# Holding back GpSimd's gathers until the other engines have moved on, in a macaron block (expert FFN, scan, expert FFN)

## The chip, the cores and the metric

The kernel runs on one core of one Trainium2 chip. The metric is device time in microseconds (us) of one execution, given as the median of three runs. All times below are from the kernel before the change.

## The reference

The block is x + 0.5·FFN(norm x), then x + Attn(norm x), then x + 0.5·FFN(norm x) again, with the same FFN weights, on 4 × 512 tokens of 256 floats. The FFN has a shared expert and 16 routed ones of width 176, of which each token uses four.

```python
def _L0_ffn_ref(x, ...):
    scores = jax.nn.sigmoid(logits) + gate_b
    weights, indices = jax.lax.top_k(scores, 4)
    weights = weights / weights.sum(-1, keepdims=True)
    shared_out = jax.nn.silu(x @ w1_shared) * (x @ w3_shared) @ w2_shared
    ...
    h3 = jax.nn.silu(h1 * h2)
    experts_out = jnp.einsum('btec,ecd->bted', h3, w2_routed)
    routed_out = jnp.einsum('bted,bte->btd', experts_out, router_probs)
    return shared_out + routed_out
# _L0_attn_ref: xp = x W_in; dt = softplus(xp W_dt + b); a = exp(-dt exp(log_A));
# y_t = a_t * y_(t-1) + xp_t over the 512 tokens; output y W_out
x = x + 0.5 * _L0_ffn_ref(_layernorm(x, axis=-1), ...)
x = x + _L0_attn_ref(_layernorm(x, axis=-1), ...)
x = x + 0.5 * _L0_ffn_ref(_layernorm(x, axis=-1), ...)
```

## The kernel before, in words

Tokens stand in 16 token tiles of 128 rows (`NT`), resident in SBUF as `xres`. Each of the two FFN layers (`f` = 0 and 1) has the same stages. The block is written out by hand for five engines: each engine has its own program, in the order of the code, and they meet only at semaphores. Nothing reorders it.

**Routing.** The tokens are normed, written to DRAM (`xn_scratch`), and sorted by expert into at most 79 slot tiles (`NS`) of 128 rows, each for one expert.

**The loop over 79 slot tiles** (`pipeline`). GpSimd gathers the rows of slot tile j with an indirect DMA into one of `UN` = 4 buffers (`gather`, L555). TensorE transposes them (L1387, counted by `s_xt`, "x_transposed"), multiplies by the expert's up weights (L1365, counted by `s_h`), transposes the hidden values (L1426 and L1427) and multiplies by the down weights (L1416). In one step c of its pipeline TensorE does, in this order: transpose of tile c, up product of tile c−1, down product of tile c−4, hidden transposes of tile c−2. ScalarE's step holds, in order: the first copy of hidden values (L671, counted by `s_a`, "hidden_first"), the copy of transposed hidden values (L662), of transposed rows (L653), the silu (L702) and the copy of the output (L681). VectorE forms the products and the low halves of the operands. SyncE writes each output tile to DRAM (`ys_scratch`).

**Early rows.** A token tile's result is the weighted sum of four rows of `ys_scratch` per token. For the first 8 token tiles this is begun inside the loop: from gather 29 on, behind every second gather, GpSimd also issues one `fetch_early` (L567), 25 of 32 in the loop and 7 behind it. VectorE adds them to `xres` (L1100, counted by `s_ea`).

**Behind the loop** GpSimd runs `combine` for the other 8 token tiles, t = 8 to 15, here called k = 0 to 7: four gathers each (L580), 32 in all. In layer 0 the scan part (called mamba in the code) runs beside them on the other engines, in 9 chunks c of two or one token tiles: ScalarE norms (L854), TensorE transposes (L1574, `m_s["xt"]`), ScalarE copies (L862, then `xin`), TensorE multiplies (L1582, `m_s["xp"]`), ScalarE copies (L868), TensorE multiplies (L1582, `m_s["z"]`), then ScalarE's chain of functions, VectorE's scan and TensorE's output product (L1607). There are six rooms for the gathered rows, so k = 6 and 7 wait for VectorE's additions (L1143, counted by `s_cd`). In layer 1, what runs beside the gathers is the shared expert's down part, in 8 pairs of token tiles: TensorE transposes (L1491, `s_st`), ScalarE copies (L752, counted by `s_hs`), TensorE multiplies (L1502, `s_sy`), VectorE adds (L1165), and VectorE adds the gathered rows (L1143). There each k has a room of its own, and the gathers wait for nothing but their first release. Each finished token tile goes out by a DMA.

A gather waits in GpSimd's own program, so everything behind it in that program waits too.

Of the kernel before, what the change touches and what calls it, by code (L numbers as in the profile page):

```python
# [12 lines left out]
NT = N // P  # L13
# [7 lines left out]
UN = 4  # L21
NS = NSLOT_MAX
NT_TE = -(-NS // UN) * UN
STEPS = NT + NS
# [14 lines left out]
ROOMS = 6  # L39
# [2 lines left out]
MEASURED = 5  # L42
SCALED = ((0, 4), (4, EARLY_TILES))
TABLE_AFTER = 76
SH_BEFORE, SH_ENDS = 2, 11
HID_AHEAD = 6
SUMS_AFTER = {9: (0, 1), 10: (2,), 11: (3,), 12: (4,), 13: (5,), 14: (6, 7)}
# [34 lines left out]
def build(nc, x_d, w13r_d, w2r_d, w13s_d, w2s_d, wm_d, cst_d, hcst_d, out_d):  # L82
# [7 lines left out]
    with ctx:  # L90
# [431 lines left out]
        def _(pool):  # L522
# [28 lines left out]
            def gather(f, j):  # L551

                if j >= UN:
                    pool.wait_ge(s_xt, f * STEPS + NT + j - UN + 1)
                pool.indirect_dma_start(xg[j % UN], None, xn_dram,  # L555
                                        bass.IndirectOffsetOnAxis(ap=tokidx[:, j:j + 1], axis=0)
                                        ).then_inc(s_g[j % UN], 16)

            def fetch_early(f, n):

                t, q = divmod(n, TOPK)
                if q == 0:
                    for b in range(2):
                        pool.wait_ge(s_yw[b], written(f, b, tiles_before(t)))
                if n >= ROWS:
                    pool.wait_ge(s_ea, f * EARLY + n - ROWS + 1)
                pool.indirect_dma_start(early_rows[n % ROWS], None, ys_dram[0:tiles_before(t) * P, :],  # L567
                                        bass.IndirectOffsetOnAxis(ap=si[:, n:n + 1], axis=0)
                                        ).then_inc(s_er[n % ROWS], 16)

            def combine(f, t):

                for b in range(2):
                    pool.wait_ge(s_yw[b], written(f, b, tiles_before(t)))
                if f == 0 and t >= EARLY_TILES + ROOMS:
                    pool.wait_ge(s_cd, combined_to(f, t - ROOMS))
                for q in range(TOPK):
                    n = t * TOPK + q
                    room = cgl[t - EARLY_TILES] if f else cg[(t - EARLY_TILES) % ROOMS]
                    pool.indirect_dma_start(room[:, q, :], None, ys_dram[0:tiles_before(t) * P, :],  # L580
                                            bass.IndirectOffsetOnAxis(ap=si[:, n:n + 1], axis=0)
                                            ).then_inc(gathered(f, t, q)[0], 16)
# [1083 lines left out]
```

## Time and profile before

| what | us |
|---|---|
| median of three runs | 677.86 (675.02 to 683.16) |
| the profiled execution | 680.63 |
| its span in the trace | 678.7 |
| TensorE busy in it | 523.3 (77%) |
| VectorE busy | 444.3 (65%) |
| ScalarE busy | 374.9 (55%) |
| GpSimd busy | 350.3 (52%) |

In the trace PE is TensorE, DVE is VectorE, ACT is ScalarE, POOL is GpSimd and SP is SyncE. A row of a timeline gives start, duration, engine, line, operation, what is written and read, how many instructions were merged, and in brackets the idle time of the engine before it and what ended it. "remote" there, and "another core or an unknown queue" in the chain, mean that a semaphore was reached at a time at which the trace knows no instruction that ended. Ends of matmuls are modelled.

### The profile page before, as it was taken

What the parts mean: (1) busy time and instruction counts of PE and PEld (TensorE: products, weight loads), DVE (VectorE), ACT (ScalarE), POOL (GpSimd) and SP (SyncE); (2) the same over time, 40 slices, a digit from 0 to 9 for tenths busy, and PEclk for the clock granted to TensorE, in tenths of its full rate; (3) what the DMA queues carried; (4) which work ended last, traced back from release to release, by engine and by line L of the source; (5) the groups of instructions that cost most, each with busy time, mean ns of one, the idle gap of its engine ahead of it and who ended that gap; (6) DMA issues with size and microseconds to landing.
All of it is one profiled execution on the core that took longest, in us unless ns stands there. A gap on an engine that the chain in (4) does not pass through costs nothing.

```text
span 678.7 us, 13762 instructions
## 1 busy us (share of the span) xinstructions
PE 523.3 (77%) x3206; PEld 459.5 (68%) x3207; DVE 444.3 (65%) x1461; ACT 374.9 (55%) x1128; POOL 350.3 (52%) x362
## 2 busy tenths in 40 slices
PE   4965869999999997645686932699999999978424
PEld 3843569998888887524574921499988888867313
DVE  6789747777676765513987589477666666745514
ACT  2764747766566664435575553477666666644000
POOL 3895564466565653571402323544565665644770
PEclk9977679999999998786898965699999999979655
DMA  9951135565544443431200450254444445545541
GB/s 299 393 218 47 48 111 170 157 174 151 162 132 145 136 135 98 128 107 32 63 0 17 154 187 0 63 149 140 132 141 138 146 133 145 129 114 155 160 120 67
DMA packets 61141, 88.17 MB, mean 130 GB/s; under 512 B 9499, under 2 KB 46363, under 8 KB 61107
## 3 DMA queue, kind: packets, MB, share of 16 engines
q1 hardware_dynamic: 47379, 50.29, 21.6%
q0 software_dynamic: 13728, 37.50, 21.3%
q8 instruction: 12, 0.20, 0.1%
q14 instruction: 22, 0.18, 0.1%
HBM read 57.22 MB, written 30.54 MB: 129 GB/s over the span
## 4 chain that ended last, share of the span: by engine, by line
PE 60%; DVE 12%; another core or an unknown queue 10%; ACT 8%; issue 6%; DMA 2%; POOL 1%; ACTq 0%; SPq 0%; DVEq 0%
PE bank L1365 26%; PE bank L1416 12%; PE bank L1387 6%; PE bank L1426 4%; PE bank L1427 4%; PE bank L1582 3%; PE bank L1502 2%; ACT ring_f L702 1%; PE bank L1607 1%; PE bank L1438 1%; DVE xres L1143 1%; DMA ring_f<-xn_scratch,tokidx 1%; DMA raw_shared<-in_w13s 1%; DVE stage L998 1%
## 5 line engine op out<-in xcount | busy, mean ns | idle before, releaser
L555 POOL DMA_INDIRECT ring_f<-xn_scratch,tokidx x158 | 152.5, 965 | 148.7 <-PE bank L1387 106.7
L1365 PE MATMUL bank<-w_routed,ring_r 128*128 x948 | 196.4, 343 | 0.0
L1365 PEld LDWEIGHTS bank<-w_routed,ring_r 128*128 128x128 f32 x948 | 153.3, 193 | 4.6 <-issue 2.8
L1416 PE MATMUL bank<-w_routed,ring_r 128*128 x790 | 120.1, 282 | 1.0 <-ACT ring_f L681 0.6
L1416 PEld LDWEIGHTS bank<-w_routed,ring_r 128*128 128x128 f32 x790 | 110.9, 189 | 1.8 <-issue 1.8
L662 ACT ACTIVATE ring_r<-bank 128x256 fp32r<-128x256 f32 x158 | 60.6, 384 | 63.3 <-PE bank L1427 51.1
L671 ACT ACTIVATE stage<-bank 128x176 f32<-128x176 f32 x158 | 50.4, 319 | 54.6 <-PE bank L1365 28.7
L947 DVE TENSOR_TENSOR ring_r<-bank,ring_r 128x128 fp32r<-128x128 f32 x158 | 45.3, 287 | 51.8 <-ACT ring_r L662 50.6
L580 POOL DMA_INDIRECT mamba_room<-ys_scratch,si x64 | 61.0, 953 | 33.1 <-issue 19.6
L939 DVE TENSOR_TENSOR ring_r<-bank,ring_r 128x256 fp32r<-128x256 f32 x158 | 67.0, 424 | 15.8 <-ACT ring_r L653 8.6
L1387 PE MATMUL bank<-cst,ring_f 128*128 128x128 f32 x316 | 64.9, 288 | 14.6 <-DMA ring_f<-xn_scratch,tokidx 10.4
L524 POOL TENSOR_TENSOR w_routed<-raw_routed,w_routed 128x512 fp32r<-128x512 f32 (+1 forms) x36 | 54.2, 1539 | 33.6 <-ACT w_routed L637 33.6
L653 ACT ACTIVATE ring_r<-bank 128x256 fp32r<-128x256 f32 x158 | 60.4, 383 | 19.9 <-issue 9.8
L956 DVE TENSOR_TENSOR ring_f<-bank,stage 128x48 f32<-128x48 f32 x158 | 32.6, 206 | 59.0 <-ACT stage L671 44.9
L702 ACT ACTIVATE ring_f<-ring_f 128x240 f32<-128x240 f32 x158 | 63.6, 402 | 0.3 <-DVE ring_f L957 0.2
L681 ACT ACTIVATE ring_f<-bank 128x256 f32<-128x256 f32 x158 | 60.0, 380 | 4.1 <-DMA ys_scratch<-ring_f 2.1
L1426 PE MATMUL bank<-cst,ring_f 128*128 128x128 f32 x158 | 46.3, 293 | 18.5 <-ACT ring_f L702 13.2
L1582 PE MATMUL bank<-mamba_room,stage 128*128 128x256 f32 (+1 forms) x144 | 39.1, 423 | 26.6 <-ACT mamba_room L862 15.6
L1387 PEld LDWEIGHTS bank<-cst,ring_f 128*128 128x128 f32 x316 | 38.3, 145 | 25.8 <-issue 13.5
L1582 PEld LDWEIGHTS bank<-mamba_room,stage 128*128 128x128 f32 x144 | 28.8, 221 | 35.5 <-ACT mamba_room L862 16.2
L957 DVE TENSOR_TENSOR ring_f<-bank,stage 128x176 f32<-128x176 f32 x158 | 52.1, 330 | 0.0
L949 DVE TENSOR_TENSOR ring_r<-bank,ring_r 64x128 fp32r<-64x128 f32 x158 | 46.5, 294 | 2.1
(172 smaller groups left out, 836.2 us busy)
## 6 DMA issues: line engine op xcount, KB each, us to landing
ys_scratch<-ring_f SPq DMA_DIRECT2D x158, 128.0 KB
raw_routed<-in_w13r SPq DMA_DIRECT2D x6, 704.0 KB, 12.1
xn_scratch<-w_routed SPq DMA_DIRECT2D x32, 128.0 KB, 4.5
raw_routed<-in_w2r SPq DMA_DIRECT2D x6, 512.0 KB, 12.9
raw_routed<-in_w13r SPq DMA_DIRECT2D x8, 352.0 KB, 6.2
ring_f<-xn_scratch,tokidx POOLq DMA_INDIRECT x158
xres<-in_x_in SPq DMA_DIRECT2D x4, 512.0 KB, 7.1
raw_routed<-in_w2r SPq DMA_DIRECT2D x8, 256.0 KB, 7.2
```

Of the source, the lines that this page charges most:

```text
L555: pool.indirect_dma_start(xg[j % UN], None, xn_dram, bass.IndirectOffsetOnAxis(ap=tokidx[:, j:j + 1], axis=0)).then_inc(s_g[j % UN], 16)
L580: pool.indirect_dma_start(room[:, q, :], None, ys_dram[0:tiles_before(t) * P, :], bass.IndirectOffsetOnAxis(ap=si[:, n:n + 1], axis=0)).th ...
L653: act.activation(xT[b][0], p_xT[b][:, 0:DC * P], ACT.Copy).then_inc(s_xhi, 1)
L662: act.activation(hT[b][0], p_hT[b][:, 0:2 * P], ACT.Copy).then_inc(s_hhi, 1)
L681: act.activation(yb[b], p_y[b][:, 0:D], ACT.Copy).then_inc(s_yo, 1)
L702: act.activation(hid[c % 2][:, 0:HD + HB], hid[c % 2][:, 0:HD + HB], ACT.Silu).then_inc(s_s, 1)
L939: dve.tensor_tensor(xT[b][1], p_xT[b][:, 0:DC * P], xT[b][0].bitcast(f32), ALU.subtract).then_inc(s_xlo, 1)
L1365: last = pe.matmul(out, a, b, start=(q == 0), stop=(q == len(terms) - 1))
L1387: last = pe.transpose(p_xT[b][:, q * P:(q + 1) * P], xg[k][:, q * P:(q + 1) * P], ident)
L1416: last = pe.matmul(p_y[b][:, 0:D], a, v, start=(q == 0), stop=(q == 4))
L1426: pe.transpose(p_hT[b][:, 0:P], hid[b][:, 0:P], ident)
L1582: last = pe.matmul(out[:, part(c, e)], m_w[m][:, q * D + e * P:q * D + (e + 1) * P], src[:, part(c, q)], start=(q == 0), stop=(q == DC - 1))
```

## The change

GpSimd gets more to wait for, at three places. No instruction is added, removed or moved on any engine.

1. In the loop, each gather j from 30 on also waits until `s_a` has reached j − 4, that is, until ScalarE's first copy of slot tile j − 5 is done. A `fetch_early` inside the loop waits for the same count as the gather ahead of it (for the first, that of gather 29).
2. Behind the loop of layer 0, the gathers of k = 1 to 5 each also wait for the scan part: k = 1 for the first chunk transposed, k = 2 for the first `xp`, k = 3 for the first `z`, k = 4 for the second `z`, k = 5 for the third `xp`.
3. Behind the loop of layer 1, those of k = 2 to 7 also wait for ScalarE's copy of pair k − 2 of the shared hidden values (`s_hs` at k − 1), and from k = 3 on for VectorE to have added all rows of k − 3.

```diff
+MAMBA_FIRST = {1: ("xt", 1), 2: ("xp", 1), 3: ("z", 1), 4: ("z", 2), 5: ("xp", 3)}
...
                 if j >= UN:
                     pool.wait_ge(s_xt, f * STEPS + NT + j - UN + 1)
+                if j > EARLY_FIRST:
+                    pool.wait_ge(s_a, f * STEPS + NT + j - UN)
...
                 if n >= ROWS:
                     pool.wait_ge(s_ea, f * EARLY + n - ROWS + 1)
+                if early_after(n) < NS:
+                    pool.wait_ge(s_a, f * STEPS + NT + early_after(n) - UN)
...
-                if f == 0 and t >= EARLY_TILES + ROOMS:
-                    pool.wait_ge(s_cd, combined_to(f, t - ROOMS))
+                k = t - EARLY_TILES
+                if f == 0:
+                    if k in MAMBA_FIRST:
+                        reached, chunks = MAMBA_FIRST[k]
+                        pool.wait_ge(m_s[reached], chunks)
+                    if k >= ROOMS:
+                        pool.wait_ge(s_cd, combined_to(f, t - ROOMS))
+                elif k >= 2:
+                    pool.wait_ge(s_hs, k - 1)
+                    if k >= 3:
+                        pool.wait_ge(s_cd, combined_to(f, t - 3))
```

GpSimd's program in the loop of layer 0, at the first early rows, before (`ring_f` is the buffer of a slot tile's rows; `stage` and `lg` are rooms of early rows):

```order
L555 DMA ring_f<-xn_scratch,tokidx 128x256 [waits x_transposed] x26
L567 DMA stage<-ys_scratch,si 128x256 [waits y_written1,y_written0]
L555 DMA ring_f<-xn_scratch,tokidx 128x256 [waits x_transposed] x2
L567 DMA stage<-ys_scratch,si 128x256
L555 DMA ring_f<-xn_scratch,tokidx 128x256 [waits x_transposed] x2
```

and the same place after:

```order
L558 DMA ring_f<-xn_scratch,tokidx 128x256 [waits x_transposed] x26
L572 DMA stage<-ys_scratch,si 128x256 [waits hidden_first,y_written1,y_written0]
L558 DMA ring_f<-xn_scratch,tokidx 128x256 [waits hidden_first,x_transposed] x2
L572 DMA stage<-ys_scratch,si 128x256 [waits hidden_first]
L558 DMA ring_f<-xn_scratch,tokidx 128x256 [waits hidden_first,x_transposed] x2
```

The order is the same; every transfer behind the first 30 gathers has a wait more, for ScalarE's count.

GpSimd's program behind the loop of layer 0, k = 0 to 5, before (`mamba_room` holds the gathered rows):

```order
L580 DMA mamba_room<-ys_scratch,si 128x256 [waits y_written1,y_written0,y_sums]
L580 DMA mamba_room<-ys_scratch,si 128x256 x3
L580 DMA mamba_room<-ys_scratch,si 128x256 [waits y_written1,y_written0]
L580 DMA mamba_room<-ys_scratch,si 128x256 x3
L580 DMA mamba_room<-ys_scratch,si 128x256 [waits y_written1,y_written0]
```

and after:

```order
L594 DMA mamba_room<-ys_scratch,si 128x256 [waits y_written1,y_written0,y_sums]
L594 DMA mamba_room<-ys_scratch,si 128x256 x3
L594 DMA mamba_room<-ys_scratch,si 128x256 [waits m_xt,y_written1,y_written0]
L594 DMA mamba_room<-ys_scratch,si 128x256 x3
L594 DMA mamba_room<-ys_scratch,si 128x256 [waits m_xp,y_written1,y_written0]
L594 DMA mamba_room<-ys_scratch,si 128x256 x3
L594 DMA mamba_room<-ys_scratch,si 128x256 [waits m_z,y_written1,y_written0]
L594 DMA mamba_room<-ys_scratch,si 128x256 x3
L594 DMA mamba_room<-ys_scratch,si 128x256 [waits m_z,y_written1,y_written0]
```

Here too nothing moved: the first gather of each four has a wait more, on a count of TensorE.

## Rows read from the trace of the kernel before

**Rows 1.** The page: busy time by engine, and the chain's shares.

```profile
PE 523.3 (77%) x3206; PEld 459.5 (68%) x3207; DVE 444.3 (65%) x1461; ACT 374.9 (55%) x1128; POOL 350.3 (52%) x362
...
PE 60%; DVE 12%; another core or an unknown queue 10%; ACT 8%; issue 6%; DMA 2%; POOL 1%; ACTq 0%; SPq 0%; DVEq 0%
```

**Rows 2.** The waits: us in total, times, longest.

```profile
ACT raw_ring L752 <- remote: 33.2, 2, 25.3
...
DVE xres L1165 <- remote: 18.3, 2, 16.1
...
ACT mamba_room L862 <- remote: 16.7, 1, 16.7
```

**Rows 3.** Windows, L671 alone (one per slot tile): length, busy (count), PEclk, DMA share, GB/s.

```profile
441.00:481.00 40.00, 6.38 (x20) 1.00 0.49 142
500.00:590.00 90.00, 11.96 (x38) 1.00 0.48 139
...
160.00:250.00 90.00, 12.06 (x38) 1.00 0.50 145
```

**Rows 4.** Timeline of GpSimd in the loop of layer 1.

```profile
520.14 0.95 POOL L555 DMA_INDIRECT ring_f<-xn_scratch,tokidx  x1 [1.28 <-PE bank L1387]
521.39 0.95 POOL L567 DMA_INDIRECT stage<-ys_scratch,si  x1 [0.30 <-issue]
522.64 0.95 POOL L555 DMA_INDIRECT ring_f<-xn_scratch,tokidx  x1 [0.30 <-issue]
524.86 0.94 POOL L555 DMA_INDIRECT ring_f<-xn_scratch,tokidx  x1 [1.27 <-PE bank L1387]
```

**Rows 5.** The same stretch, TensorE and ScalarE.

```profile
523.40 0.27 PE L1427 MATMUL bank<-cst,ring_f 128*128 128x128 f32 x1
523.51 0.38 PE L1387 MATMUL bank<-cst,ring_f 128*128 128x128 f32 x2
...
523.65 1.22 PE L1365 MATMUL bank<-w_routed,ring_r 128*128 x6
524.66 0.38 ACT L662 ACTIVATE ring_r<-bank 128x256 fp32r<-128x256 f32 x1 [1.27 <-PE bank L1427]
...
525.76 0.33 ACT L671 ACTIVATE stage<-bank 128x176 f32<-128x176 f32 x1
```

**Rows 6.** Timeline of GpSimd behind the loop of layer 0: gathers 1, 16 and 24.

```profile
279.55 0.94 POOL L580 DMA_INDIRECT mamba_room<-ys_scratch,si  x1 [0.30 <-issue]
...
298.32 0.95 POOL L580 DMA_INDIRECT mamba_room<-ys_scratch,si  x1 [0.30 <-issue]
...
308.33 0.94 POOL L580 DMA_INDIRECT mamba_room<-ys_scratch,si  x1 [0.30 <-issue]
```

**Rows 7.** The same stretch, TensorE and ScalarE.

```profile
293.14 1.99 PE L1582 MATMUL bank<-mamba_room,stage 128*128 128x256 f32 x8 [1.27 <-ACT mamba_room L868]
295.31 0.66 PE L1574 MATMUL bank<-cst,mamba_room 128*128 128x128 f32 x4 [0.17 <-ACT mamba_room L854]
...
311.92 0.60 ACT L862 ACTIVATE mamba_room<-bank 128x512 f32<-128x512 f32 x1 [16.66 <-remote]
```

**Rows 8.** Timelines of TensorE, ScalarE, VectorE and GpSimd, end of layer 1.

```profile
629.79 0.60 PE L1491 MATMUL bank<-cst,mamba_room 128*88 128x128 f32 x4
...
658.07 3.78 PE L1502 MATMUL bank<-raw_shared,raw_ring 88*128 88x256 f32 x8 [18.05 <-issue]
...
666.54 7.19 PE L1502 MATMUL bank<-raw_shared,raw_ring 88*128 88x256 f32 x16 [3.84 <-ACT raw_ring L752]
...
657.42 0.59 ACT L752 ACTIVATE raw_ring<-bank 88x512 f32<-88x512 f32 x1 [25.33 <-remote]
665.90 1.08 ACT L752 ACTIVATE raw_ring<-bank 88x512 f32<-88x512 f32 x2 [7.88 <-remote]
...
647.68 2.05 DVE L1143 SCALAR_TENSOR_TENSOR xres<-mamba_room,wk,xres 128x256 f32<-128x256 f32 x4
...
656.21 0.95 POOL L580 DMA_INDIRECT mamba_room<-ys_scratch,si  x1 [0.30 <-issue]
```

## Prediction

> **What bounds the kernel now.** I read the page first. TensorE is busy for 77% of the span and carries 60% of the chain, but 10% of the chain, some 67 us, belongs to no instruction the trace knows [rows 1]. The waits say where the long pieces of it are: ScalarE's L752 and VectorE's L1165 near the end, and ScalarE's L862 in the scan part, each for 16 to 25 us at a stretch and ended by "remote" [rows 2]. All three wait on TensorE. The reader is to ask whether TensorE was late, and it was not. In the scan part its transposes L1574 ended at 295.97, and ScalarE, idle since 295.26, copied their result at 311.92, 16 us later [rows 7]. Near the end the transposes L1491 ended at 630.39 and their copy began at 657.42, 27 us later [rows 8].
>
> Next I looked at what ran meanwhile. In the first stretch GpSimd issued 24 gathers without a break, 1.25 us apart, the last ending at 309.27, and ScalarE came free 2.65 us after that [rows 6, 7]. In the loop the same stands small. A slot tile takes 2.00 us while GpSimd issues one gather for each, and 2.37 us once every second gather has an early row behind it, in both layers [rows 3]. A pair then takes 4.74 us instead of 4.00. In it GpSimd issues three transfers in a row, 520.14 to 523.59 [rows 4]. TensorE's hidden transposes ended at 523.67, and ScalarE took them at 524.66, 1.07 us after GpSimd had stopped; GpSimd itself, which waited for transposes that ended at 523.89, went on at 524.86 [rows 4, 5]. So my reading: while GpSimd issues gathers back to back, TensorE's progress reaches the others late, and it comes through some 1 to 2.6 us after GpSimd pauses. The trace shows the coincidence, not the cause.
>
> **Part 1, the loop.** The gate adds a wait and no work. Before, a pair was three transfers (3.45 us from first start to last end), 1.07 us until TensorE's progress was seen, and 0.20 us until GpSimd went on: 4.72, which fits the 4.74. Queued behind a gated gather on GpSimd are the next early row and gather; TensorE waits for them only if the four buffers run dry, and a gather is needed four steps, 8 us, after the transpose that freed its room.
> The gain at most: if the pauses fall so that nothing is seen late, the pair returns to 4.00. Tiles 25 to 72 are 24 pairs in each layer, so 0.74 × 24 × 2 = 35.5 us. The loss: the gate needs ScalarE's copy behind the up product, a 0.33 us instruction [rows 5], instead of TensorE's transpose. If that product too is seen 1.07 us after GpSimd stops, the pair is 3.45 + 1.07 + 0.33 + 0.30 (the shortest gap between two transfers, taken for the way back [rows 4]) = 5.15, so 0.41 × 48 = 20 us more. Between them lies a mixture. Three transfers every 4.00 us leave GpSimd a pause of only 0.55 us, less than the 1.07 that followed a row of three, which speaks against a full cure; TensorE can run ahead of a longer pair, which speaks against the full loss. I take 0, nearest to the row of before, and keep −35 and +20.
>
> **Part 2, behind the loop of layer 0.** GpSimd's k = 0 to 3 end at 299.27 [rows 6]; what k = 1 to 3 wait for (the first chunk) is done well before. k = 4 needs the second z, whose matmuls ended at 295.13 [rows 7], but GpSimd learns that as late as ScalarE does. So I expect GpSimd to stop at 299.27, TensorE's progress to come through at most 2.65 us later, and ScalarE's L862 to start at 301.9 instead of 311.92: 10.0 us earlier. From this I take 1 us off, because k = 4 and 5 now run beside the next chunk, where before GpSimd was silent, and a row of three cost 1.07. That is −9. If z is seen promptly, the gate holds only at k = 5 (third xp, which needs the stalled L862): GpSimd stops 5 us later, at 304.3, and the gain is 5. If pauses free nothing, it is 0. What the gate delays costs nothing: k = 4 and 5 are added two and more chunks later, and k = 6 and 7 waited for additions already. Bounds −10 and 0.
>
> **Part 3, behind the loop of layer 1.** Seven of the eight gates are open in time in the timeline of before: for the closest of those of VectorE, k = 7 starts at 656.21 and VectorE had added k = 4 at 649.73 [rows 8]. The copy that k = 7 asks for (pair 5) began at 657.42. GpSimd stops at 655.9, and the copy, now freed within 1 to 2.6 us of that, stays near 657.4 to 658. The gathers of k = 7 start about 2 us later. But the silence frees the copy of pair 6 too, which before came only at 665.90, since its transposes were long done. TensorE's last three products are then one row: from 658.1, 3.78 us for pair 5, 1.06 for the last transposes at that pace, and 7.19 for pairs 6 and 7 [rows 8], ending at 670.1. Before, they ended at 673.73. So −3.6. Bounds: −8 if ScalarE is freed as early as 653, +2 if only the 2 us of delay are left.
>
> **A rule against the change.** GpSimd's gathers share the DMA engines with everything else, and those are busy for 0.48 to 0.49 of the time in the quick stretch and in the slow one alike [rows 3]. The Trainium skill, "DMA: Bandwidth & Descriptors", section "SWDGE vs HWDGE vs iDMA", says that queues fed by software and by hardware are separate inside each DMA engine and served in turn. By that, gathers cannot shut others out of the engines, and spacing them frees no transfer: the time would be that of the second rival below. The trace agrees on the equal DMA share; it does not say whether semaphores suffer in another way.
>
> **The sum.** 0 − 9 − 3.6 = −12.6 us on the profiled execution, 680.63 to 668.0 (its span 678.7 to 666.1). The median of the three runs stands 2.8 us below that execution, so the forecast is 665.3, rounded to 665.
>
> **The rivals.**
> - *The loop is cured in part or in whole.* For it speaks that the pair was 4.00 us with single gathers [rows 3], and that the gate stops GpSimd exactly when ScalarE is behind. Against it: the 0.55 us pause. Half the cure is −18 on top: 647. The whole is 630.
> - *The pauses free nothing.* The late semaphores have another cause, which only happens to end near GpSimd's pauses; the copy at 657.42 came while GpSimd was still issuing [rows 8], which speaks for it. Then the gates hold a little here and there behind work that is late anyway: 677.9, give or take 3. Against it are the 1.07 us in the loop, at every pair.
> - *The gate feeds back and the kernel is slower.* At the loop's third transfer, TensorE's up product is seen late, ScalarE's copy follows, and only then the next gather: 5.15 us a pair. That costs 20 us and outweighs the 12.6: 685. It decides from 0.26 us more a pair (12.6 / 48). For it speaks that GpSimd has no slack to give (three transfers 1.25 us apart in a pair of 4.00); against it, that TensorE has 8 us of buffers.
>
> Also possible is that a gate simply never holds, since GpSimd asks for counts that are nearly always reached; in parts 2 and 3 that is the second rival.
>
> **How the numbers follow.** The forecast 0.42, the cure 0.20, nothing freed 0.20, the feedback 0.18. The range goes half way into the cure's values and up to the feedback's, 642 to 684; the forecast's own is 656 to 672. A measurement of this kernel can tell about 1%, 6.8 us, from no change. Faster by more: 0.38 of the forecast's 0.42, the cure's 0.20 and 0.04 of the second rival, 0.62. Slower by more: 0.16 of the feedback and 0.02 of the second, 0.18. Within 1%: the rest, 0.20.
>
> **What would show it.** In the changed profile, L862's 16.7 us and L752's 33.2 us under "remote" should fall to a few us each; a pause of GpSimd should stand ahead of k = 4 in layer 0 and ahead of k = 7 in layer 1, and ScalarE's wait should end 1 to 2.6 us into it. The count of L671 in 90 us of the loop tells part 1: 38 is no change, 45 the cure, 35 the feedback. If the count moves by more than 1, part 1's zero was wrong. If GpSimd pauses and ScalarE still waits over 5 us into the pause, my reading of the cause is wrong.

## The result, and the profile after

| | us |
|---|---|
| changed kernel, median | 710.95 (702.01 to 716.08, 4 runs) |
| kernel before, beside it | 679.63 (675.02 to 683.16, 4 runs) |
| ratio | 1.0365, 95% interval 1.0311 to 1.0419 |
| profiled execution of the changed kernel | 707.15, its span 705.3 |

The ratio and its interval compare the kernel before with the changed kernel's 702.01 and 707.15 alone, since 714.75 and 716.08 fell in a slower state that some executions of either kernel can show; the median of 710.95 takes in all four. By the ratio the kernel became 3.7% slower. The forecast was 665, so the sign was wrong. The rival that came true is the third, the gate that feeds back. Lines in the changed file stand 14 further down for TensorE, ScalarE and VectorE (L671 is L685), and GpSimd's gathers are L558 (loop), L572 (early rows) and L594 (behind the loops).

The page of the changed kernel, against [rows 1]:

```profile
PE 524.7 (74%) x3206; PEld 468.4 (66%) x3207; DVE 446.8 (63%) x1461; ACT 374.9 (53%) x1128; POOL 350.9 (50%) x362
...
PE 56%; DVE 12%; another core or an unknown queue 11%; issue 9%; ACT 8%; DMA 2%; POOL 1%; ACTq 0%; SPq 0%; DVEq 0%; POOLq 0%
```

The work is the same to within 3 us on every engine (TensorE's weight loads, PEld, which overlap its products, have 8.9 us more), and the span is 26.6 us longer: nearly all of it is waiting. From the first to the last of ScalarE's first copies, the loop of layer 0 takes 191.8 us in place of 177.8, that of layer 1 193.6 in place of 179.4; what lies between the loops takes 1.7 us less, and what follows the last copy takes the same (63.5 and 63.4). So the loops, 28.2 us longer together, have more than all of it. The windows, L685 alone, against [rows 3]:

```profile
441.00:481.00 40.00, 5.39 (x17) 0.90 0.44 126
500.00:590.00 90.00, 10.47 (x33) 0.92 0.40 120
160.00:250.00 90.00, 10.74 (x34) 0.98 0.44 129
```

Where 38 slot tiles went by in 90 us, now 33 or 34 do: 2.7 us each in place of 2.37, in both layers. (The first window lies in the stretch of single gathers and has 17 in place of 20 only because the loop of layer 1 now begins at 448.23; the single gathers still come 2.00 us apart.) The prediction set 35 for the feedback and 38 for no change. The waits:

```profile
POOL ring_f L558 <- ACT stage L685: 39.9, 21, 2.0
...
ACT ring_r L676 <- remote: 32.7, 10, 4.3
...
ACT raw_ring L766 <- remote: 37.6, 3, 21.9
...
DVE xres L1179 <- remote: 16.1, 2, 15.9
...
ACT mamba_room L882 <- remote: 14.2, 2, 10.5
```

The first is the new gate, but only a part of it: a wait for several counts is put down to the one that the profile sees last. Held against ScalarE's copies one by one, 55 of the 98 gathers with the new wait start 0.74 to 0.76 us after the end of just the copy that they ask for, and these are all that waited at all; some stand in the profile as waits for TensorE. The second, ScalarE's copy of transposed hidden values in the loop, was this before:

```profile
ACT ring_r L662 <- remote: 9.1, 2, 5.8
```

The third and fourth are the waits of the last stage, 33.2 and 18.3 us before [rows 2], and together they have not shrunk.

One turn of the loop shows the feedback. GpSimd in the late loop of layer 1:

```profile
532.78 0.95 POOL L558 DMA_INDIRECT ring_f<-xn_scratch,tokidx  x1 [1.95 <-ACT stage L685]
534.04 0.95 POOL L572 DMA_INDIRECT stage<-ys_scratch,si  x1 [0.30 <-issue]
535.29 0.95 POOL L558 DMA_INDIRECT ring_f<-xn_scratch,tokidx  x1 [0.30 <-issue]
538.09 0.95 POOL L558 DMA_INDIRECT ring_f<-xn_scratch,tokidx  x1 [1.85 <-ACT stage L685]
539.34 0.94 POOL L572 DMA_INDIRECT stage<-ys_scratch,si  x1 [0.30 <-issue]
540.59 0.95 POOL L558 DMA_INDIRECT ring_f<-xn_scratch,tokidx  x1 [0.30 <-issue]
541.84 0.95 POOL L558 DMA_INDIRECT ring_f<-xn_scratch,tokidx  x1 [0.30 <-issue]
543.09 0.95 POOL L572 DMA_INDIRECT lg<-ys_scratch,si  x1 [0.30 <-issue]
547.14 0.94 POOL L558 DMA_INDIRECT ring_f<-xn_scratch,tokidx  x1 [3.10 <-PE bank L1401]
```

and the copy that the gate asks for, with the product ahead of it on TensorE:

```profile
534.02 1.23 PE L1379 MATMUL bank<-w_routed,ring_r 128*128 x6
...
537.02 0.32 ACT L685 ACTIVATE stage<-bank 128x176 f32<-128x176 f32 x1 [1.97 <-remote]
...
544.49 0.38 ACT L676 ACTIVATE ring_r<-bank 128x256 fp32r<-128x256 f32 x1 [3.59 <-remote]
...
546.08 0.32 ACT L685 ACTIVATE stage<-bank 128x176 f32<-128x176 f32 x1
```

The up product ended at 535.25, while GpSimd was between two transfers. GpSimd's row of three ended at 536.24, and only 0.78 us after that did ScalarE take the product. Its copy ended at 537.34, and the next gather started 0.75 us later. So the pair took 3.46 (the row) + 0.78 + 0.32 + 0.75 = 5.31 us, the sum of the rival with its terms a little shifted (3.45 + 1.07 + 0.33 + 0.30). After a pause the opposite comes: counts that have piled up let five transfers through in a row (538.09 to 544.04). While they run ScalarE waits 3.59 us for TensorE's hidden transposes and takes them 0.45 us after the row; its next first copy ends at 546.40, and 0.74 us later GpSimd goes on, at 547.14. The profile names TensorE for that wait of 3.10 us, but the time is the gate's. Three slot tiles have then taken 9.05 us, where 7.1 were usual. The gates do not spread the transfers. They bunch them.

### The profile page after: what moved, and what is told of

The parts are those of the page before. It is cut to its first block, busy times and chain, and to the rows that moved or that the text cites. A ratio compares the mean times of both kernels' runs of the same rounds, so it can differ in the third digit from the quotient of the medians.

```text
span 705.3 us, 13903 instructions
## 1 busy us (share of the span) xinstructions
PE 524.7 (74%) x3206; PEld 468.4 (66%) x3207; DVE 446.8 (63%) x1461; ACT 374.9 (53%) x1128; POOL 350.9 (50%) x362
## 4 chain that ended last, share of the span: by engine, by line
PE 56%; DVE 12%; another core or an unknown queue 11%; issue 9%; ACT 8%; DMA 2%; POOL 1%; ACTq 0%; SPq 0%; DVEq 0%; POOLq 0%
PE bank L1379 24%; PE bank L1430 13%; PE bank L1401 5%; PE bank L1440 3%; PE bank L1441 2%; PE bank L1596 2%; ACT ring_f L716 2%; PE bank L1516 2%; DMA ring_f<-xn_scratch,tokidx 1%; DVE lg L933 1%; PE bank L1621 1%; DMA raw_shared<-in_w13s 1%; DVE stage L1012 1%; ACT ring_r L667 1%
## 5 line engine op out<-in xcount | busy, mean ns | idle before, releaser
L558 POOL DMA_INDIRECT ring_f<-xn_scratch,tokidx x158 | 153.0, 969 | 182.0 <-PE bank L1401 101.4
L1379 PE MATMUL bank<-w_routed,ring_r 128*128 x948 | 201.9, 350 | 4.4 <-issue 2.8
L1379 PEld LDWEIGHTS bank<-w_routed,ring_r 128*128 128x128 f32 x948 | 158.1, 199 | 10.9 <-issue 9.8
L1430 PE MATMUL bank<-w_routed,ring_r 128*128 x790 | 123.6, 288 | 0.7 <-DVE ring_r L963 0.6
L1430 PEld LDWEIGHTS bank<-w_routed,ring_r 128*128 128x128 f32 x790 | 114.4, 195 | 1.6 <-issue 1.6
L685 ACT ACTIVATE stage<-bank 128x176 f32<-128x176 f32 x158 | 50.1, 317 | 46.1 <-PE bank L1379 26.4
L594 POOL DMA_INDIRECT mamba_room<-ys_scratch,si x64 | 61.3, 958 | 23.2 <-issue 19.0
L1596 PE MATMUL bank<-mamba_room,stage 128*128 128x256 f32 (+1 forms) x144 | 36.9, 405 | 26.8 <-issue 13.9
L1440 PEld LDWEIGHTS bank<-cst,ring_f 128*128 128x128 f32 x158 | 22.5, 142 | 48.7 <-ACT ring_f L716 45.8
L1401 PEld LDWEIGHTS bank<-cst,ring_f 128*128 128x128 f32 x316 | 40.3, 148 | 16.8 <-DMA ring_f<-xn_scratch,tokidx 12.3
```

What stands on the lines that cost most here:

```text
L558: pool.indirect_dma_start(xg[j % UN], None, xn_dram, bass.IndirectOffsetOnAxis(ap=tokidx[:, j:j + 1], axis=0)).then_inc(s_g[j % UN], 16)
L1379: last = pe.matmul(out, a, b, start=(q == 0), stop=(q == len(terms) - 1))
L1401: last = pe.transpose(p_xT[b][:, q * P:(q + 1) * P], xg[k][:, q * P:(q + 1) * P], ident)
L1430: last = pe.matmul(p_y[b][:, 0:D], a, v, start=(q == 0), stop=(q == 4))
L1440: pe.transpose(p_hT[b][:, 0:P], hid[b][:, 0:P], ident)
L1596: last = pe.matmul(out[:, part(c, e)], m_w[m][:, q * D + e * P:q * D + (e + 1) * P], src[:, part(c, q)], start=(q == 0), stop=(q == DC - 1))
```

## What the experiments were to tell apart

The kernel before took 677.9 to 686.8 us in some groups of runs and 602 in others. The groups of experiments fell on four numbered chips (that of the first profiles is not on record). Chip 1 gave the same time in both of its groups; the other three had one group each, so that it is the chip, and not the hour, rests on these five groups. Each comparison below is within one group.

| chip | kernel before | runs on it |
|---|---|---|
| 12 | 686.83 (684.39 to 689.59) | e1 to e4 |
| 9 | 602.71 (600.43 to 607.51) | e5 to e8 |
| 1 | 679.09 (673.16 to 682.31) | f1 to f4 |
| 2 | 601.63 (600.92 to 605.50) | g1 to g4 |
| 1 | 680.53 (673.21 to 681.54) | h1, h2 |

On chips 12 and 1, as in the profiles above, single waits ended by "remote" last up to 28.9 us (e1, e3 and e4) and up to 19.8 (f1). In the eight profiles from chips 9 and 2 the views of waits have no "remote" at all. I call the first two late chips and the others prompt chips.

## Which part of the change costs

**e1_loop_gates**, the change without its parts behind the loops:

```diff
+                if j > EARLY_FIRST:
+                    pool.wait_ge(s_a, f * STEPS + NT + j - UN)
...
+                if early_after(n) < NS:
+                    pool.wait_ge(s_a, f * STEPS + NT + early_after(n) - UN)
```

> Only the gates inside the two loops, none behind them. Feedback theory (ScalarE's copy lies behind TensorE's late progress, so each row of transfers starts later): both loops as long as in the changed kernel, 14 us more each than before, slot tiles 2.65 to 2.75 us apart instead of 2.37, total +26 to +30 us against before. Rival (the gates behind the loops cost the time, or the loop only lengthens together with them): under +10 us.

**e2_behind_gates**, the change without these two waits.

> Only the gates behind the loops. Feedback theory: loops as before (178 and 179 us from first to last copy). Behind the loop of layer 0 the gate at the fifth group of four stops GpSimd and frees ScalarE, but the sixteen gathers then issued in a row hold it again: -5 to +2 us; layer 1 unchanged within 2 us. Total -6 to +3. Rival (part 2 works as I forecast and only the loop spoilt the result): -8 to -13 us.

**e3_looser**, e1 with the count one lower in both (`- UN - 1`), so that the copy asked for is one slot tile older.

> Loop gates alone, each asking for one copy less (that of slot tile j-6 instead of j-5). Feedback theory: that copy is done before GpSimd would start anyway, so the gate hardly holds: within 5 us of before. Rival (any extra wait on GpSimd costs, whatever it asks for): as much as the loop gates as they are, +20 or more.

**e4_rows_gate**, e1 with the gate on the early rows alone, none on the gathers.

> Of the loop gates only those of the early rows are left; the gathers of slot tiles are free. Feedback theory: the early row still waits for the copy and stands between two gathers, so most of the loss stays, though not at each gather: +8 to +20 us. Rival (the loss comes from the slot tiles' gathers reaching TensorE too late): 0 to +4.

| | median us | ratio, 95% interval | both loops in the profile, us |
|---|---|---|---|
| e1_loop_gates | 724.09 (722.18 to 725.72) | 1.0543 (1.0507 to 1.0579) | 395.6 |
| e2_behind_gates | 679.19 (677.26 to 687.22) | 0.9908 (0.9875 to 0.9940) | 361.5 |
| e3_looser | 701.43 (701.19 to 703.05) | 1.0204 (1.0172 to 1.0237) | 377.8 |
| e4_rows_gate | 691.73 (688.81 to 694.54) | 1.0060 (1.0032 to 1.0088) | 371.6 |

The last column adds the two loops, each from its first to its last first copy; e2's are without a gate. The loop's gates cost 37 us alone, more than the 26 to 30 that I had expected, and 34 of them stand in the loops' own length. The gates behind the loops give back 6 by the ratio and 8 by the medians, between e2's two expectations (6 at most by the one, 8 at least by the other). Together that is 30, near what the change cost on chip 1 (32 and 30 us by the ratios below; 25 in its first group). e4 costs 4 us by the ratio, where I had expected 8 to 20, though its profile, of its slowest execution, has loops 10 us longer: two of the three transfers of a pair are free of the gate there, so the early rows' gate is the small part and the gathers' the large one. For e3 I had expected little or no cost, and it costs 14 us. GpSimd in its late loop says why:

```profile
526.03 0.94 POOL L558 DMA_INDIRECT ring_f<-xn_scratch,tokidx  x1 [1.02 <-PE bank L1392]
527.28 0.95 POOL L572 DMA_INDIRECT stage<-ys_scratch,si  x1 [0.30 <-issue]
528.53 0.95 POOL L558 DMA_INDIRECT ring_f<-xn_scratch,tokidx  x1 [0.30 <-issue]
531.61 0.94 POOL L558 DMA_INDIRECT ring_f<-xn_scratch,tokidx  x1 [2.13 <-ACT stage L676]
...
541.84 0.94 POOL L558 DMA_INDIRECT ring_f<-xn_scratch,tokidx  x1 [2.12 <-ACT stage L676]
```

The gate still holds, but in every second pair: two pairs take 10.2 us (531.61 to 541.84) where two of [rows 4] take 9.48. One copy of slack halves how often the loop closes and does not open it.

## Are the gathers what makes TensorE late?

**e5_rows_by_memset** and **f3_rows_by_memset** are one kernel. Every early row is zeros from GpSimd, so the early rows' sums are left out:

```diff
-                pool.indirect_dma_start(early_rows[n % ROWS], None, ys_dram[0:tiles_before(t) * P, :],
-                                        bass.IndirectOffsetOnAxis(ap=si[:, n:n + 1], axis=0)
-                                        ).then_inc(s_er[n % ROWS], 16)
+                pool.memset(early_rows[n % ROWS], 0.0).then_inc(s_er[n % ROWS], 16)
```

**e6_late_by_memset** and **f4_late_by_memset** do the same to the gathers behind both loops, and leave out those sums:

```diff
-                    pool.indirect_dma_start(room[:, q, :], None, ys_dram[0:tiles_before(t) * P, :],
-                                            bass.IndirectOffsetOnAxis(ap=si[:, n:n + 1], axis=0)
-                                            ).then_inc(gathered(f, t, q)[0], 16)
+                    pool.memset(room[:, q, :], 0.0).then_inc(gathered(f, t, q)[0], 16)
```

> The kernel before, with one edit: each early row (64 in all, 50 of them in the loops) is filled with zeros by a memset on GpSimd instead of being gathered, so the early rows' sums are left out; VectorE's additions of them stay. Theory (TensorE's progress is seen late while GpSimd issues gathers one behind the other): the rows of three gathers are gone, the pair of slot tiles returns from 4.74 toward 4.00 us, the count of L671 in 90 us of the late loop goes from 38 to 44 or 45, and the kernel is 25 to 36 us shorter, some 650 on the median of before. Rival A (VectorE's additions of the early rows, or GpSimd being busy with anything, slow the loop): the count stays at 38 to 39, and the time falls by under 8 us, through the 14 gathers behind the loops that no longer stand ahead of the others. Rival B (the data that the early rows move is what slows the loop): as the theory in time, but then the count would also be below 45 in the early part of the loop where the transfers share is the same, 0.48 to 0.50, which it is not; so this run tells the gathers from all else on GpSimd and VectorE, not their issue from their data.

> The kernel before, with one edit: the rows added behind both loops (32 gathers in each layer) are zeros from a memset on GpSimd, so that part of the routed sum is left out; VectorE's additions stay. This is the ceiling for anything that could be done about those gathers. Theory: TensorE's progress is seen at once, ScalarE's long waits (16.7 us at L862, 33.2 us at L752 and VectorE's 18.3 us at L1165) fall below 3 us each, and the kernel is 20 to 35 us shorter, some 650. Rival (the late progress has another cause than the gathers, as the weights or the outputs on their queues): the long waits stay above 10 us each, and the time falls by under 8 us.

> Early rows filled with zeros by a memset on GpSimd in place of their gathers, so the early rows' sums are left out. Theory (rows of gathers hold TensorE's progress back, on a chip that shows it): if the kernel before is near 680 here, the pair returns from 4.74 to within 0.1 of 4.00 us and the ratio is 0.95 to 0.965. Rival (the late loop is slow there for another reason, as VectorE's additions or the chip's clock): the ratio is above 0.99. Where the kernel before is near 603 this says nothing new (1.00 again).

> The gathers behind both loops replaced by a memset, so those parts of the routed sum are left out. Where the kernel before is near 603 the ratio was 0.965, some 20 us, which is what these gathers cost with TensorE's progress seen at once. Theory: if the kernel before is near 680 here, the long waits under remote add to that, and the ratio is 0.91 to 0.94 (20 us and the 68 us under remote of rows 2, less what overlaps). Rival (the long waits have nothing to do with these gathers): 0.965 to 0.975, and the waits stay.

| what is replaced | prompt chip 9 | late chip 1 |
|---|---|---|
| early rows | e5: 604.60, 1.0016 (0.9986 to 1.0047) | f3: 629.15, 0.9272 (0.9210 to 0.9334) |
| rows behind both loops | e6: 583.19, 0.9647 (0.9604 to 0.9691) | f4: 629.44, 0.9281 (0.9230 to 0.9332) |

On a prompt chip the early rows cost nothing. On a late chip the same 64 transfers cost 50 us, more than the 24 to 34 that f3's ratio of 0.95 to 0.965 expected; the pair itself came back to 3.99 us, as expected. The rows behind the loops cost 20 us of GpSimd's plain work on the one and 50 on the other. If the two savings add, which no run tried, the late progress is worth 50 + 30 = 80 us of the kernel before, and the two sorts of chip lie 76 to 85 us apart: these gathers would account for the whole distance. ScalarE's first copies in the loops, f3 (L669), against [rows 3]:

```profile
160.00:250.00 90.00, 14.40 (x45) 1.00 0.47 132
```

There are 45 slot tiles in 90 us where [rows 3] has 38, on a late chip, with all 158 gathers of the loops still in place. So it is not GpSimd's gathers as such. That it is a second and third one close behind them, f3 alone does not show, since the rows it takes away are also the ones read from `ys_scratch`; h2 below keeps every gather and only spaces them. And the two long waits behind the loops, which f3 leaves alone, are still there, while f4 has neither:

```profile
ACT raw_ring L750 <- remote: 25.4, 1, 25.4
...
ACT mamba_room L860 <- remote: 16.4, 1, 16.4
```

What a prompt chip does with a row of three gathers is in e8_paced, whose loop is that of before:

```profile
229.45 0.94 POOL L556 DMA_INDIRECT ring_f<-xn_scratch,tokidx  x1 [0.54 <-PE bank L1395]
230.70 0.95 POOL L568 DMA_INDIRECT raw_shared<-ys_scratch,si  x1 [0.30 <-issue]
231.96 0.95 POOL L556 DMA_INDIRECT ring_f<-xn_scratch,tokidx  x1 [0.30 <-issue]
233.44 0.94 POOL L556 DMA_INDIRECT ring_f<-xn_scratch,tokidx  x1 [0.54 <-PE bank L1395]
```

The instructions, their order and their durations are those of [rows 4]. GpSimd goes on after 0.54 us in place of 1.27, and the pair is 3.99 us. What it waits for is this:

```profile
232.79 0.38 PE L1395 MATMUL bank<-cst,ring_f 128*128 128x128 f32 x2
```

These transposes ended at 233.17, 0.27 us before the gather at 233.44. On the late chip they ended at 523.89 and the gather came at 524.86, 0.97 us behind [rows 4, 5]. The DMA engines were busier in that loop (0.60 of the time from 160 to 250 us, against 0.50), and nobody was late. The rule that I had weighed against the change, the Trainium skill's "DMA: Bandwidth & Descriptors", section "SWDGE vs HWDGE vs iDMA", that queues fed by software and by hardware are separate within a DMA engine, is untouched by this: no run shows a gather keeping another transfer out. The time that I drew from it, that of the second rival, did not come. What is held back is word of TensorE's progress.

**f1_before_traced** is the kernel before, unchanged, for a profile on chip 1, and **f2_change_again** and **h1_change_third** are the change, unchanged.

> The kernel before, unchanged, for a profile on the chip of this group of runs. On the chip of the first group of experiments the kernel before took 686.8 us, on that of the second 602.7, with a slot tile at 2.00 us where before it was 2.37. Expected: either some 680 with L671 at 38 in 90 us of the late loop and long waits under remote, or some 603 with 45 and none of them; nothing between. If it is the second, the late progress of TensorE belongs to a chip and not to this program.

> The change as it is, on this group's chip. Theory (the gates cost what they do because ScalarE's first copy, which they ask for, is itself held up by late progress of TensorE): if this chip shows the late progress (kernel before near 680), the ratio is again 1.02 to 1.04; if it does not (near 603), the gates of the loop hold for little, a pair of slot tiles stays within 0.05 us of 4.00, and the ratio is 0.995 to 1.015, the rest coming from the gates behind the loops. Rival (the gates cost by themselves, with no late progress: the copy comes too late in the step for a gather to be issued in time): the pair grows by 0.3 us or more on either chip and the ratio is 1.02 or more on both.

> The change as it is. Kernel before near 603: by the theory (the gates cost through late progress) a pair of slot tiles stays within 0.1 us of 4.00 and the ratio is 1.00 to 1.015; by the rival (the gates cost by themselves, since ScalarE's first copy comes late in the step) the pair grows by 0.3 us or more and the ratio is 1.025 or more. Kernel before near 680: 1.04 again.

f1 took 679.92 us, and its longest "remote" waits are 17.4 us at L862 and 19.8 at L752, as in [rows 2]. f2 took 709.84, ratio 1.0478 (1.0411 to 1.0545), and h1 709.17, 1.0447 (1.0368 to 1.0526). Both fell on chip 1. Both ratios lie at or above the upper end of what was expected (1.02 to 1.04, and 1.04). What the change costs on a prompt chip was never measured, so the rival that the gates also cost by themselves is not excluded there. The expectation of f2 that they hold for little on such a chip is doubtful: in e8's loops, which have no gate, the 98 gathers start up to 2.1 us before the end of the copy that the gate would ask for, and none after it.

## Does a pause let the progress through?

In the change every pause hangs on a count that is itself late. These kernels pause on other grounds.

**g1_pauses_behind** and **h2_pauses_behind** are one kernel: a pause of fixed length, by filling with zeros, twice, the room that the next four gathers then overwrite.

```diff
+            def pause(dst, n):
+                for _ in range(n):
+                    pool.memset(dst, 0.0).then_inc(s_p, 1)
+                    paused[0] += 1
+                    pool.wait_ge(s_p, paused[0])
...
+                if f == 0 and k >= 1:
+                    pause(room, 2)
+                if f == 1 and k in (2, 4, 6):
+                    pause(room, 2)
```

> The kernel before, with pauses of fixed length behind the loops: in layer 0 ahead of each k from 1 to 7, in layer 1 ahead of k = 2, 4 and 6, GpSimd fills the room of that k with zeros twice (some 2 to 2.6 us), which the gathers then overwrite; nothing of another engine is waited for. On a chip that shows the late progress (kernel before near 680) the theory (a pause lets it through) expects L862's single wait of 17 us at no more than some 8 (four gathers and a pause), L752's of 20 to 25 at no more than some 12, and a ratio of 0.97 to 0.99. Rival (a pause lets nothing through by itself; the progress comes when the gathers are over): the waits stay at 16 us and more or grow by the pauses, and the ratio is 1.00 to 1.02. On a chip that does not show it: 1.00 to 1.01 by either.

> The same kernel as g1_pauses_behind. Kernel before near 680: by the theory (a pause lets the held progress through) ScalarE's single waits under remote behind the loops are at most some 12 us and the ratio is 0.97 to 1.00; by the rival (it comes only when the gathers are over) they keep 16 us or more and the ratio is 1.00 to 1.03. Kernel before near 603: 1.03 again, the price of the pauses themselves.

On the prompt chip g1 took 621.50, ratio 1.0308 (1.0252 to 1.0365): ten pauses of 2 us cost 20 us there, where I had expected 0 to 6. On the late chip the same kernel, h2, took 667.20, ratio 0.9851 (0.9773 to 0.9929): 10 us faster than before by the ratio, although the pauses are as long. Its waits:

```profile
ACT raw_ring L766 <- remote: 5.5, 1, 5.5
```

This is the only wait under "remote" behind the loops that is left; L862's 17.4 us and L1165's 15.4 of f1, on the same chip, are gone. GpSimd in its scan part:

```profile
291.64 0.95 POOL L594 DMA_INDIRECT mamba_room<-ys_scratch,si  x1 [0.30 <-issue]
292.58 1.98 POOL L556 MEMSET mamba_room<- 128x1024 f32 x2
294.83 0.95 POOL L594 DMA_INDIRECT mamba_room<-ys_scratch,si  x1 [0.27 <-POOL mamba_room L556]
...
298.59 0.94 POOL L594 DMA_INDIRECT mamba_room<-ys_scratch,si  x1 [0.30 <-issue]
299.53 1.98 POOL L556 MEMSET mamba_room<- 128x1024 f32 x2
```

and ScalarE's copies of the transposes beside it:

```profile
295.34 0.60 ACT L876 ACTIVATE mamba_room<-bank 128x512 f32<-128x512 f32 x1 [0.75 <-PE bank L1588]
...
302.11 0.60 ACT L876 ACTIVATE mamba_room<-bank 128x512 f32<-128x512 f32 x1 [0.75 <-PE bank L1588]
```

With a pause every 7 us a chunk goes through every 7 us, and ScalarE's wait is 0.75 us where it was 16.66 [rows 7]. GpSimd was busy writing zeros in these pauses. So what matters is that it issues no gather for some 2 us, not that it idles. Whether it is the issuing of the gathers or the moving of their rows that stops in such a pause, no run separates.

**e7_landing** and **g4_landing** are one kernel, in which GpSimd waits, behind both loops, ahead of every second k for the landing of the four gathers before:

```diff
+                if t > EARLY_TILES and t % 2 == 0:
+                    for q in range(TOPK):
+                        pool.wait_ge(*gathered(f, t - 1, q))
```

> The kernel before, with one edit: behind both loops GpSimd waits ahead of k = 2, 4 and 6 until the four gathers ahead of it have landed, so it pauses after every 8 gathers for the time that a gather takes to land, about 2 us or more; what it waits for has nothing to do with TensorE. Theory (any pause of about 1 to 2.65 us lets the late progress through): ScalarE's single waits under remote are no longer than some 11 us (8 gathers at 1.25 us and the pause) in place of 16.7 and 25.3, and the kernel is 5 to 15 us shorter, near 667. Rival (the pauses free nothing, the progress of TensorE is late for as long as its own cause lasts): the waits keep their 16 to 25 us and the time is that of before or up to 5 us longer.

> The same kernel as e7_landing: behind the loops GpSimd waits ahead of k = 2, 4 and 6 until the four gathers before have landed. On a chip that shows the late progress: theory, no single wait under remote is longer than 11 us there and the ratio is 0.975 to 0.995; rival, the waits keep 16 to 25 us and the ratio is 1.00 to 1.02. On a chip that does not: 1.02 again.

e7 took 615.33, ratio 1.0199 (1.0141 to 1.0257), and g4 614.75, 1.0190 (1.0132 to 1.0248), both on prompt chips: the price of such pauses without their use.

**e8_paced** and **g3_paced** are one kernel, without gates in the loops and with the gates behind them laid otherwise:

```diff
-MAMBA_FIRST = {1: ("xt", 1), 2: ("xp", 1), 3: ("z", 1), 4: ("z", 2), 5: ("xp", 3)}
+MAMBA_FIRST = {1: ("xt", 1), 2: ("xp", 1), 3: ("z", 1), 4: ("z", 2), 5: ("z", 3), 6: ("z", 4), 7: ("z", 5)}
...
                 elif k >= 2:
-                    pool.wait_ge(s_hs, k - 1)
-                    if k >= 3:
-                        pool.wait_ge(s_cd, combined_to(f, t - 3))
+                    pool.wait_ge(s_hs, min(k + 4, NT // 2))
```

> No gates in the loops. Behind the loop of layer 0 the gates are spread over seven token tiles (k = 1: first chunk transposed, 2: first xp, 3 to 7: first to fifth z), behind that of layer 1 those of k = 2 to 7 ask for ScalarE's copies of min(k + 4, 8) pairs alone. Theory (a gate pays where it keeps the rows of gathers short while TensorE's results are wanted): layer 0's row of 16 gathers behind the gate of k = 4 is cut into fours, ScalarE's wait of 10.6 us there falls to some 6, and in the tail the copies of pairs 5 to 7 are no longer behind 28 gathers; together 5 to 15 us less than before, 1 to 2% (some 668 to 673). Rival (each gate asks for progress that is itself seen late, so it hands back what it frees): within 4 us of the kernel before, or slower, as the change's own gates behind the loops (0.991) allow.

> The same kernel as e8_paced. On a chip that shows the late progress: theory, the waits under remote in the scan part fall to some 6 us and those in the tail to under 15, ratio 0.975 to 0.99; rival (the gates hand back what they free), ratio 0.99 to 1.01. On a chip that does not: 1.01 again.

e8 took 609.83, ratio 1.0099 (1.0066 to 1.0133), and g3 608.43, 1.0108 (1.0044 to 1.0172), on prompt chips both. On a late chip it did not run.

**g2_pauses_in_loop** puts a pause into the loops only, between an early row's gather and the next:

```diff
+                if any(early_after(n) == j - 1 for n in range(EARLY)):
+                    pause(xg[j % UN], 3)
```

> The kernel before, with a pause of fixed length in the loops only: between each early row's gather and the gather behind it GpSimd fills the buffer of that gather with zeros three times (some 1.0 to 1.5 us), which the gather overwrites. It cuts the row of three transfers into two and one. Theory: TensorE's progress is seen about 1.1 us after the second transfer as well, so TensorE no longer loses the whole 0.74 us per pair; but GpSimd has 3 x 1.25 and some 1.3 us to issue in a pair, so the pair is 4.7 to 5.1 us and the ratio 1.00 to 1.03. Rival (the row does not matter, only that three transfers and their 1.07 us are in a pair): 4.72 and the pause of 1.0 to 1.5 on top, 5.7 to 6.2 us, a ratio of 1.06 to 1.10. On a chip that does not show it: the pair is bound by GpSimd's own 5 us and the ratio is near 1.07, since 4.00 was the pair there.

It fell on a prompt chip: 637.42, ratio 1.0570 (1.0507 to 1.0632). There GpSimd's own work sets the pair. Whether such a pause helps on a late chip is open. No version here beats both kernels on both sorts of chip; on late chips h2 does, and e2 by a little.

## Why the prediction was wrong, point by point

**The reading of the bound was right.** TensorE's progress reaches the others late while GpSimd issues gathers back to back, and comes through once it pauses. f3 and f4 show the first half by taking the gathers away, h2 the second by pausing alone. What I had called a coincidence in the trace is a cause, on these chips. The second rival, pauses free nothing, is refuted by h2. But a pause is not the only thing that lets progress through: the copy at 657.42 [rows 8], one at 643.91 in e2 and one at 681.14 in the changed kernel came while GpSimd was issuing, and why is open.

**Part 1 is the step that failed.** I took 0 for the loop, between −35.5 and +20, as "nearest to the row of before". It was +28.2 us in the changed kernel's own profile, and +37 when alone (e1). The mechanism stood among the rivals, with 5.15 us for a pair; single turns of the loop came to 5.31, and over 90 us 33 slot tiles give 2 × 90 / 33 = 5.45. The rows on record told that the gate must hold. The gather at 524.86 [rows 4] is one whose new wait is for the copy that ended at 526.09 [rows 5], 1.23 us after that gather had started, and in the trace of before all 98 gathers with the new wait start ahead of their copy's end, by 0.35 to 2.9 us. My reason against it, that TensorE has 8 us of buffers, counted the buffers and not what fills them: GpSimd issues three transfers a pair and had 1.27 us to spare of 4.74, and the gate put ScalarE's 0.32 us and a way back of 0.75 into just that time. The way back was also mis-sized, taken as 0.30 from a gap in which GpSimd waited for nobody. And nothing bounded the time by 20: after every second or third wait counts had piled up, and rows of five followed, worse than the three that I had reckoned with (9.05 us for three slot tiles). In the windows TensorE's granted clock was also lower, 0.98 in layer 0 and 0.92 in layer 1 where it had been 1.00, full speed, and TensorE was busy for 75.9 of 90 us in the late loop of layer 1 in place of 85.0. Its products took a little longer: L1379 has a mean of 350 ns where L1365 had 343, over 948 of them 5.5 us busy.

**Part 2 had the mechanism and missed what comes behind it.** I expected GpSimd to stop ahead of k = 4, and ScalarE to be freed within 2.65 us of it: −9. GpSimd and ScalarE of the changed kernel, behind the loop of layer 0:

```profile
311.86 0.94 POOL L594 DMA_INDIRECT mamba_room<-ys_scratch,si  x1 [0.31 <-issue]
316.43 0.94 POOL L594 DMA_INDIRECT mamba_room<-ys_scratch,si  x1 [3.62 <-remote]
...
335.67 0.95 POOL L594 DMA_INDIRECT mamba_room<-ys_scratch,si  x1 [0.30 <-issue]
```

```profile
315.72 0.60 ACT L876 ACTIVATE mamba_room<-bank 128x512 f32<-128x512 f32 x1 [4.75 <-remote]
...
337.61 0.60 ACT L882 ACTIVATE mamba_room<-bank 128x512 f32<-128x512 f32 x1 [10.53 <-remote]
```

GpSimd did stop at 312.80, and ScalarE went on at 315.72, 2.92 us later. Its wait was 4.75 us in place of 16.66. But k = 4 to 7 then formed one row of 16 gathers, 316.43 to 336.62, since no gate behind that of k = 4 held. ScalarE took two more copies early in that row, at 319.00 and 322.49, and then lost 10.53 us at the next, which came 0.99 us after the row. Most of what the release had gained was lost again in the row that it let loose. e2 repeats it: 6.7 us at L872 and 10.6 at L878. From layer 0's last first copy of hidden values to layer 1's first the two traces differ by 1.7 us (164.4 and 162.7): the term should have been near −2, not −9.

**Part 3 did not come.** I had k = 7 held by its gate, and −3.6. (I also counted eight gates there; the code has eleven waits, at six places.) In the changed kernel GpSimd's gathers run from 647.12 to 687.54 without a pause, no gate holding, and ScalarE's wait was 21.86 us. The copy of pair 5 came at 681.14, in the middle of the row and just ahead of k = 7, due at 682.84, so there was no pause to free pair 6:

```profile
681.14 0.59 ACT L766 ACTIVATE raw_ring<-bank 88x512 f32<-88x512 f32 x1 [21.86 <-remote]
692.42 1.08 ACT L766 ACTIVATE raw_ring<-bank 88x512 f32<-88x512 f32 x2 [10.68 <-remote]
```

In e2, whose loops have no gate, that of k = 7 did hold, for 6.33 us from 658.52 on. What ended it was VectorE's addition of k = 4, which I had called open in time, and ScalarE's copy came at 662.86, 4.34 us into the pause, where I had 1 to 2.6. Parts 2 and 3 together gave −6.3 us (0.9908 on 686.8) where I had −12.6. Half of that term was right, with the right sign.

**The chances.** The feedback had 0.18, though it was the only rival that cost time and had a sum of its own. The loop's 48 pairs carry every error per pair 48 times, and a range that ended at 684, just under the rival's own 685, left no room above it for a rival that was itself too small.

## What to carry to other kernels

Before a wait is added so that an engine "doesn't run ahead", see whether the thing waited for is itself held up by that engine: then the wait closes a loop, and its price is paid each turn. A throttle that asks for counts releases in bursts; where rows of transfers are what hurts, a pause of known length between short rows did what the counts did not (h2 against e2). And a wait of 16 us under "remote", on an engine whose producer ended long before, says to look at what a third engine was issuing meanwhile, and to measure on more than one chip before tuning for it.

## What the runs showed of the hardware

I had not expected that the same program takes 602 us on two chips and 679 to 687 on two others, with TensorE's granted clock 1.00 in loops without gates on both (e8; f1 and e2). With single gathers at 2.00 us per slot tile the loop of a late chip is as quick as that of a prompt one (f3: 45 in 90 us). With rows of three transfers GpSimd goes on 0.97 us after the end of the transposes that it waits for on a late chip and 0.27 on a prompt one (1.27 and 0.54 after its own last transfer), and with the row of 32 behind the loop of layer 1 up to 27 us after TensorE's end on the one [rows 8], while the profiles of the other have no wait under "remote". Why chips differ so, what ends a hold while GpSimd goes on issuing, and which link between GpSimd's issuing and TensorE's counts is the slow one, no run here shows.
